# A loop over image pairs written out as straight code, with constant wait counts, in a convolution and codebook kernel

## The reference

```python
LL, LH, HL, HH = haar(groupnorm(x))                     # 64 x 64 bands
hf = concat(LH, HL, HH)
added = conv5(act(conv5(hf))) + conv3(act(conv3(hf))) + conv2(act(conv2(hf)))   # each with act
y = three dilated 3x3 convolutions of added
phf = sigmoid(conv1(y)) * hf
z = batchnorm(conv3(concat(LL, phf)))
x = x + inverse_haar(z * sigmoid(z), conv1(phf), HL, HH)
x = x + codebook[argmin_k |groupnorm(x) - codebook[k]|^2]     # 512 codes of 32 values
```

## Time and profile before

| | us |
|---|---|
| median of 3 runs | 2288.87 |
| lowest, highest | 2281.72, 2294.78 |
| span of the profiled execution, first to last instruction | 2164.4 |
| profiled execution's own time | not given on the page |
| median less span | 124.5 |
| TensorE busy | 1984.8 (92%) |
| VectorE busy | 1810.3 (84%) |
| GpSimd busy | 1252.3 (58%) |
| ScalarE busy | 1059.2 (49%) |
| TensorE's granted clock, mean over the span | 0.951 |

### The profile page before, as it was taken

One profiled execution on the slowest core, in us unless ns is written; L12 is line 12 of the kernel. 1 busy time (PEld: TensorE's weight loads), 2 busy tenths in 40 slices (PEclk: granted clock), 3 DMA queues, 4 the chain that ended last, 5 costly groups with the idle time before them and its releaser, 6 DMA issues. The chain is left out here.

```text
span 2164.4 us, 27115 instructions
## 1 busy us (share of the span) xinstructions
PE 1984.8 (92%) x5232; PEld 946.5 (44%) x5232; DVE 1810.3 (84%) x3979; ACT 1059.2 (49%) x2018; POOL 1252.3 (58%) x1299
## 2 busy tenths in 40 slices
PE   6999999999999999999999999999999999995653
PEld 3444455444544455444544445444544445442221
DVE  4122799988999799988999899988999889888996
ACT  5134645545555545546556454546455454543331
POOL 2001277654776377663776367673776457673876
PEclk9999999999999999999999999999999999995555
DMA  6000011111110112111111111111111011110111
GB/s 203 15 10 5 20 40 43 27 29 34 46 35 21 41 36 47 25 24 41 42 36 26 42 35 41 30 24 37 43 41 26 20 25 34 30 25 20 34 37 32
DMA packets 80459, 76.97 MB, mean 36 GB/s; under 512 B 29200, under 2 KB 62608, under 8 KB 80016
## 3 DMA queue, kind: packets, MB, share of 16 engines
q1 hardware_dynamic: 45776, 50.78, 8.3%
q0 software_dynamic: 32768, 16.84, 5.2%
q10 hardware_dynamic: 1728, 7.41, 0.9%
HBM read 41.36 MB, written 16.78 MB: 27 GB/s over the span
## 5 line engine op out<-in xcount | busy, mean ns | idle before, releaser
L1053 POOL DMA_INDIRECT vqc<-in_codebook,idx x1024 | 1000.9, 977 | 545.2 <-DVE idx L964 306.4
L542 PE MATMUL ring<-hf,w_sb 128*128 128x512 f32 x1824 | 888.5, 600 | 2.9 <-ACT hf L715 2.9
L487 PE MATMUL score<-cst,yst 98*128 98x512 f32 x1024 | 788.4, 777 | 83.8 <-DVE idx L964 54.8
L960 DVE MAX8 top<-score 128x8 f32<-128x512 f32 x1024 | 695.3, 684 | 74.7 <-PE score L487 63.8
L964 DVE FIND_INDEX8 idx<-top,score 128x8 uint32<-128x512 f32 x1024 | 704.2, 690 | 0.0
L666 ACT CAST yst<-bands 32x256 fp32r<-32x256 f32 x1024 | 411.3, 402 | 174.6 <-PE score L487 162.1
L542 PEld LDWEIGHTS ring<-hf,w_sb 128*128 128x128 f32 x1824 | 341.6, 191 | 316.9 <-issue 294.2
L487 PEld LDWEIGHTS score<-cst,yst 98*128 98x128 f32 x1024 | 204.0, 202 | 395.0 <-DVE idx L964 206.3
L542 PE MATMUL ring<-ha,w_sb 128*128 128x512 f32 x704 | 347.5, 598 | 5.1 <-DVE ha L853 4.6
L542 PE MATMUL ring<-hb,w_sb 128*128 128x512 f32 x544 | 262.6, 595 | 6.8 <-DVE hb L866 6.8
L627 ACT ACTIVATE z<-ring,prm 128x512 f32<-128x512 f32 x144 | 99.0, 688 | 273.3 <-PE ring L542 272.7
(11 more groups left out here) (101 smaller groups left out, 1276.8 us busy)
## 6 DMA issues: line engine op xcount, KB each, us to landing
xnat<-in_x SPq DMA_DIRECT2D x128, 128.0 KB, 2.7
yst<-yl SPq DMA_DIRECT2D x512, 32.0 KB
vqc<-in_codebook,idx POOLq DMA_INDIRECT x1024
out<-vqc SPq DMA_DIRECT2D x128, 128.0 KB
w_sb<-in_weights ACTq DMA_DIRECT2D x1, 1920.0 KB, 8.2
w_sb<-in_weights ACTq DMA_DIRECT2D x3, 384.0 KB, 12.8
w_sb<-in_weights ACTq DMA_DIRECT2D x1, 1152.0 KB, 15.6
w_sb<-in_weights ACTq DMA_DIRECT2D x1, 960.0 KB, 8.6
```

Source lines behind the costliest of these rows:

```text
L487: nc.tensor.matmul(score[BANK["tile", t]][:, :], yst[0:KST, j % 2, g, wp], cst[0:KST, :], start=True, stop=True).then_inc(s_tile, 1)
L542: t = nc.tensor.matmul(ring[g % RING][:, :, :], w_sb[:, SLOTS[n, m, kind, ky], :], own(source(n, m, kind), half, slice(PAD + di, PAD + di ...
L960: nc.vector.max(top8[:, t % 4, :], score[BANK["tile", t]][:, :]).then_inc(s_top, 1)
L1053: nc.gpsimd.indirect_dma_start(vqc[:, c % 2, w * CH:(w + 1) * CH], None, codebook[:, :], bass.IndirectOffsetOnAxis(idx[:, c % 2, k, 0:1], ...
```

## The change

The loop is replaced by a Python loop, so bodies 1 to 6 are built one after the other with b as a number. Three pairs of bodies stand in the program in place of one; the jump back, the loop counter and the register instructions are gone; every wait of these bodies has a constant. The order of the other instructions is the same on each engine.

```diff
@@ -356,9 +356,8 @@
 
 
             body(0, 0, True, False, True)
-            with eng.Fori(0, (IMAGES - 2) // 2) as i:
-                body(2 * i + 1, 1, True, True, True)
-                body(2 * i + 2, 0, True, True, True)
+            for b in range(1, IMAGES - 1):
+                body(b, b % 2, True, True, True)
             body(IMAGES - 1, 1, True, True, False)
             body(IMAGES, 0, False, True, False)
 
```

## The result

| us | before | changed | ratio, 95% interval |
|---|---|---|---|
| median (5 runs each) | 2288.17 | 2219.57 | 0.970, 0.968 to 0.973 |
| lowest, highest | 2281.72, 2294.78 | 2218.44, 2228.22 | |
| span of the profiled execution | 2164.4 | 2217.8 | |

The change makes the kernel 3.0% faster, 68.6 us, where 3.0 us were forecast. The forecast was wrong. The table also holds a riddle: the profiled execution of the changed kernel has a *longer* span than the one of before, yet its own time is 2219.57 us, only 1.8 us above its span. So nothing like 124.5 us lies outside a span here.

What follows compares the result with a forecast made beforehand. TensorE was taken to set the pace, VectorE close behind. Jumps saved 3.0 us, register arithmetic and added code nothing: 2288.9 - 3.0 = 2285.9 us, range 2273 to 2299, no difference from no change expected at 0.84.

Steps and rivals of the forecast that it cites:

- The frame: Whole run: span 2164.4 us and median 2288.87 us used together, the 124.5 us outside the span carried over unchanged.
- Rival C: Outside the span: the longer program makes the 124.5 us there grow by a tenth, giving 2298 us; chance 0.03.
- Part 1, the jumps: Seams before images 3 and 5: removing two backward jumps saves 2.4 to 3.65 us, taken as 3.0.
- Part 2, the register arithmetic: Register instructions ahead of nearly every wait in the loop: hidden behind running work or waits, so removing them gains nothing.
- The bound of 7 us: Limit on the register arithmetic's effect over six images, either way, from TensorE's busy time in loop images and image 7.
- three agreeing comparisons: Loop against written-out image 7: max8 pace, a VectorE-to-ScalarE handoff and TensorE's busy total, read as register arithmetic costing zero.
- Part 3: Loop bodies standing three times in the program: fetching the longer straight code costs nothing.
- Rival B: Late fetches in straight code hold VectorE some 3 us once per image: +15.2 us, 2304 us; chance 0.05.
- Rival A: VectorE's 768 register instructions all exposed at 40 ns: 30.7 us less, 2255 us; chance 0.07, including a milder form.

Runs made afterwards that it cites:

- j0: The changed kernel with no further edit, run again on a quick machine: 2161.8 us, ratio 0.9978 to the kernel before.
- i2: Kernel before with the loop written out on TensorE and VectorE alone, slow machine: 2255.3 us, ratio 0.988.
- i3: Kernel before with the loop written out on ScalarE, GpSimd and SyncE alone, slow machine: 2255.5 us, ratio 0.989.
- m1: Changed kernel plus 34 semaphore increments behind each of SyncE's 128 stacks, slow machine: 2277.8 us, ratio 0.997 to the kernel before.

## Why the prediction was wrong

**The frame: wrong, and the first thing to fail.** The prediction took 2288.87 - 2164.4 = 124.5 us as time outside the span and carried it over unchanged. Every run since has 1.8 to 1.9 us there. The 124.5 us were the other condition: the trace was quick, the runs were slow. What followed from the trace was right for a quick execution and said little of the runs that were measured. Rival C, growth outside the span, had the same fault.

**Part 1, the jumps: right in mechanism and place, a little small.** The idle time ahead of bn_aggr is 0.14 us, both TensorE waits are gone, and image 2's wait is still there (2.9 us, it was 3.4). 3.0 us were forecast; on a quick machine it is 4.2 us (2.4 to 7.1 by the interval), and the span is 2160.0 us, where 2161.4 were forecast.

**Part 2, the register arithmetic: this is the term that was mis-sized.** "I price them at nothing" holds where it was read: on a quick machine the max8 pace is 1.26 us without the register instructions and 1.27 with them, and 4352 instructions more on SyncE do nothing. On a slow machine the same instructions are nearly all that the loop costs. The 4305 that went away are worth 45 to 69 us in the three sets that compare the two programs, 10 to 16 ns each; some 4 us of that are the jumps. The bound of 7 us, taken from TensorE's busy time in the quick trace, failed with the zero. Comparing the loop with image 7 inside one quick trace could not show this; three agreeing comparisons in one execution could not stand for another condition.

**Part 3: right.** In j0's trace no such hole stands before any max8, and the queues moved less, 1.47 MB. Rival B did not come.

**Rival A had the sign and the wrong mechanism.** It had VectorE's own register instructions exposed at 40 ns each. i2 and i3 refute that: writing out VectorE and TensorE is worth no more than writing out the other three, and m1 costs as much from an engine with slack. In the slow trace VectorE's additions are no longer than in the quick one. That its worked 2255 us is also what i2 and i3 took is chance.

**What stays open.** Shown is that a slow machine charges for executed instructions on SyncE and on either group of engines, that fetching is not the cause, that semaphore increments come microseconds late and in bunches, that SyncE's sequencer stands up to 1.4 us in a register addition, and that about half of the trace's semaphore updates are missing there. All this would follow if writing the trace's own records were what is overrun, with engines and increments held until there is room. That is argued and not shown: every run here, timed ones too, carries a span and a granted clock, so none was made without a recording. Whether the 3% would be there without one is not known. What brings a slow condition about is not known either, and how the charge divides between late increments and clock was not measured.

## What to carry to other kernels

Compare a profile's span with the runs' times before using it. In this kernel they lie 1.8 to 1.9 us apart; a difference of 124.5 us meant that the trace was of another condition than the runs, and was no overhead to carry over. Register arithmetic was free here on a quick machine, but the number of sequencer instructions over all engines cost percents in the other condition. Constant waits, and waits carried by the instruction that needs them, were better in both. A hole put down to issue can be a semaphore increment that came late: look at when the increments are recorded, and at the clock behind the hole. A backward jump over this long body cost VectorE some 2 us each time (2.07 and 1.86). TensorE's own took 3.3 us in its sequencer and cost the engine nothing, since queued matmuls ran meanwhile.

## What the runs showed of the hardware that was not expected

- The same program on the same chip took 2165.8 us at one time and 2289.4 us at another, at a mean granted clock of 0.95 and 0.94. In the traces of the two conditions all engines' busy sums agree within 3% (TensorE's, 1984.8 and 2031.4 us, differ most).
- 4352 more instructions on SyncE, semaphore increments alone or a third each increments, additions and branches: no cost at one time (2160.9 and 2161.3 us for 2161.8), an estimated 50 to 60 us at another (2277.8 and 2280.1 us, against 2220 to 2227 us in other sets).
- Increments of one semaphore, recorded within 20 ns of their matmuls' ends on a quick machine, came up to 3.9 us late and 50 ns apart before one max8 on a slow one; VectorE waited for them.
- Removing 2968 increments behind waits gave 12.5 us on a quick machine too, a larger gain than the whole unrolling gave there. Why is not known.
